# Experts' rows scaled on ScalarE and summed in one reduction; masked attention and quantised layer as one phase

## What is computed

```python
x = x + attn(layernorm(x))             # 16 heads of 8, causal
x = x + cross_attn(layernorm(x), ctx)  # 16 heads of 8, biases
x = x + experts(layernorm(x))          # top 2 of 8: sum of gate_i * expert_i(token)
x = x + rope_attn(layernorm(x)) + bo   # 16 heads of 64, causal, rotary
x = x + masked_attn(layernorm(x), ctx) # 1 head of 128, no weights, causal and padding mask
x = x + quantised_ffn(layernorm(x))

def quantised_ffn(x):                  # inner size 352
    xq = fake_quant(x, clip_x)         # scale = sigmoid(clip) * max|x| / 127 over the whole tensor
    h = fake_quant(silu(xq @ q(w_gate).T) * (xq @ q(w_up).T), clip_down)   # again over the whole tensor
    return h @ q(w_down).T             # q: one scale per row of the weight
```

## Time and profile before

| | |
|---|---|
| median of 3 runs (lowest to highest) | 1297.98 us (1297.2 to 1299.01) |
| the profiled execution's own time | 1297.34 us |
| its span, first to last instruction | 1295.5 us |
| busy: PE, DVE, ACT, POOL | 1035.7, 892.4, 548.0, 549.5 us |
| mean granted PE clock | 0.853 of full speed |

### The profile page before, as it was taken

One profiled execution on the slowest core, in us unless ns is written; L12 is line 12 of the kernel. 1 busy time (PEld: TensorE's weight loads), 2 busy tenths in 40 slices (PEclk: granted clock), 3 DMA queues, 4 the chain that ended last, 5 costly groups with the idle time before them and its releaser, 6 DMA issues. The chain is left out here.

```text
span 1295.5 us, 39531 instructions
## 1 busy us (share of the span) xinstructions
PE 1035.7 (80%) x14827; PEld 838.1 (65%) x14828; DVE 892.4 (69%) x2134; ACT 548.0 (42%) x877; POOL 549.5 (42%) x686
## 2 busy tenths in 40 slices
PE   2999968999935779999975999999999994661453
PEld 1566654666634679999974888888888884441112
DVE  1778764878643934444426999999999986337787
ACT  1556634666511046666632444444444442110343
POOL 3323314434220033333315888888888773103000
PEclk9999976999955579999996999999999998555555
...
DMA packets 33367, 37.54 MB, mean 29 GB/s; under 512 B 6344, under 2 KB 26507, under 8 KB 32908
## 3 DMA queue, kind: packets, MB, share of 16 engines
...
...
## 5 line engine op out<-in xcount | busy, mean ns | idle before, releaser
L1167 POOL DMA_INDIRECT e_x<-xn_rows,e_where x72 | 68.5, 951 | 202.8 <-DVE e_where L1148 116.9
L1137 DVE COPY e_y<-e_Y_ps 128x128 f32<-128x128 f32 x72 | 21.0, 291 | 109.3 <-PE e_Y_ps L1104 109.3
L1324 POOL TENSOR_TENSOR a_E<-a_E,a_rsum 128x512 f32<-128x512 f32 x64 | 66.7, 1042 | 50.7 <-DVE a_rsum L1688 50.7
L262 POOL TENSOR_SCALAR a_KX<-a_KT,a_of_head 128x512 f32<-128x512 f32 x64 | 43.0, 696 | 85.7 <-ACT a_KT L454 85.7
L1094 PE MATMUL e_G_ps<-e_xT,e_gate_here 128*128 128x128 f32 x576 | 77.9, 279 | 0.5 <-ACT e_up_here L1057 0.5
L1094 PE MATMUL e_U_ps<-e_xT,e_up_here 128*128 128x128 f32 x576 | 77.1, 277 | 0.0
L262 POOL TENSOR_SCALAR x_KX<-x_KT,x_of_head 128x512 f32<-128x512 f32 x64 | 43.1, 698 | 78.8 <-issue 49.9
L1104 PE MATMUL e_Y_ps<-m_down_w,e_hT 128*128 x576 | 76.0, 275 | 0.2 <-DVE e_hT L1155 0.2
L1056 ACT ACTIVATE e_gate_here<-m_gate_w 128x512 f32 x72 | 45.4, 630 | 70.7 <-PEq L85 44.9
L1094 PEld LDWEIGHTS e_G_ps<-e_xT,e_gate_here 128*128 128x128 f32 x576 | 71.7, 196 | 0.7 <-ACT e_up_here L1057 0.7
L1094 PEld LDWEIGHTS e_U_ps<-e_xT,e_up_here 128*128 128x128 f32 x576 | 71.2, 194 | 0.0
...
## 6 DMA issues: line engine op xcount, KB each, us to landing
...
```

What stands on the lines that cost most here:

```text
L262: last = nc.gpsimd.tensor_scalar(KX[:, p, :, h * T:(h + 1) * T], src, of_head[:, h:h + 1], 1.0, ALU.mult, ALU.mult)
L1167: nc.gpsimd.indirect_dma_start(out=x[:, j, :], out_offset=None, in_=k.xn_rows, in_offset=bass.IndirectOffsetOnAxis(ap=where[:, j, :], axis ...
L1324: nc.gpsimd.tensor_tensor(e, e, rsum[:, g % 2, :].unsqueeze(2).broadcast_to([P, GH * UB, T]), ALU.mult)\
```

## The change

`X` becomes the first of three planes of one tile, `XR`, each as large as x. Through the mixture phase all phases work in the first plane; from the wide attention on x lies in a tile of its own, `X_of_second_layer`.

In the wide attention ACT scales the gathered rows by their gates into the second and third plane (`apply_gates`, steps 0 and 1, after `evacuate_o`), and DVE sums the three planes of a block into the new x with one `tensor_reduce` whose innermost dimension is the plane (`combine`, step 2). POOL's gathers wait for `gated`, which ACT raises. Before the loop ACT scales the rows of blocks 0 and 1 before its first `normalise`.

The two last phases become `tail_phase` (prefix `t`), all of it written out without loops. Statistics go by block, in two series: series 0 for the masked attention, three blocks ahead, and series 1 for the quantised layer, of a block whose residual has just been added. Normalising moves from DVE to ACT (`centres` on DVE gives its bias), normalising E and quantising the weights go to POOL. Context loads run four blocks ahead, and the weights are loaded between the first and the second of them. In the inner layer POOL quantises x (the first block excepted, which DVE does), ACT, POOL and DVE quantise one chunk of h each, DVE clips, and POOL adds x to the output. PSUM banks of the attention serve the inner layer again, and `HT` lies in the three planes of `XR`.

```diff
@@ wide_attention_phase
-                        pool.wait_ge(combined, (nb - 1) * 2)
+                        pool.wait_ge(gated, (nb - 1) * 2)
...
+            def apply_gates(nb, i, p):
+                act.wait_ge(got[p][i], (nb // 2 + 1) * (16 * UB))
+                for u in range(UB):
+                    rows = k.XR[:, 1 + i, bass.ds(nb * UB + u, 1), :].rearrange("p o c -> p (o c)")
+                    last = nc.scalar.activation(rows, expert_rows[:, p, i, u, :], ACT.Copy, scale=k.gates[:, i, bass.ds(nb * UB + u, 1)])
+                last.then_inc(gated, 1)
...
+                for i in range(2):
+                    apply_gates(0, i, 0)
+                for i in range(2):
+                    apply_gates(1, i, 1)
                 normalise(0)
...
                     evacuate_o(blk, g)
+                    if later(nxt, 2) and g < 2:
+                        apply_gates(blk + 2, g, p)
...
-            def combine(nb, i, p):
-                if i == 1:
-                    wait_here(dve, combined, nb * 2 + 1, passed)
-                dve.wait_ge(got[p][i], (nb // 2 + 1) * (16 * UB))
-                for u in range(UB):
-                    x = k.X[:, nb * UB + u, :]
-                    last = nc.vector.scalar_tensor_tensor(out=x, in0=expert_rows[:, p, i, u, :],
-                                                          scalar=k.gates[:, i, bass.ds(nb * UB + u, 1)], in1=x,
-                                                          op0=ALU.mult, op1=ALU.add)
-                last.then_inc(combined, 1)
+            def combine(nb):
+                wait_here(dve, gated, nb * 2 + 2, passed)
+                rows = k.XR[:, :, bass.ds(nb * UB, UB), :].rearrange("p i u c -> p (u c) i")
+                nc.vector.tensor_reduce(k.X[:, bass.ds(nb * UB, UB), :].rearrange("p u c -> p (u c)"), rows, AX.X, ALU.add)\
+                    .then_inc(combined, 1)
...
-                        if g in (0, 1):
-                            combine(blk + 2, g, p)
+                        if g == 2:
+                            combine(blk + 2)
                         if g == 2:
                             statistics(blk + 2)
@@ masked_attention_phase and quantised_ffn_phase go, tail_phase comes
+    AHEAD = 4
...
+        HT = k.XR[:].rearrange("p i u c -> p i (u c)")
...
+        G_ps = S_ps
+        U_ps = [ET_ps, PV_ps[0]]
+        D_ps = [xT_ps, PV_ps[1]]
...
+            def load_ctx(nb):
+                p = nb % AHEAD
+                if nb >= AHEAD:
+                    sp.wait_ge(pv_ps, nb - AHEAD + 1)
+                sp.dma_start(ctxT[:, p, :], d["ctxT"][:, nb * TOK:(nb + 1) * TOK]).then_inc(ctx_in[p], 16)
+                sp.dma_start(ctxK[:, p, :, :], d["ctxK"][:, nb * BB:(nb + 1) * BB, :]).then_inc(ctx_in[p], 16)
+            sp.dma_start(mask[:], d["mask"]).then_inc(mask_in, 16)
+            load_ctx(0)
+            for w, name in zip(w_rows, ("L1_ffn_w_gate", "L1_ffn_w_up")):
+                for c in range(NC):
+                    sp.dma_start(w[0:ROWS[c], c, :], d[name][c * P:c * P + ROWS[c], :]).then_inc(w_in, 16)
+            sp.dma_start(w_down[:], d["L1_ffn_w_down"]).then_inc(w_in, 16)
+            sp.dma_start(clip[:], d["L1_ffn_clips"]).then_inc(w_in, 16)
+            for nb in range(1, NB):
+                load_ctx(nb)
...
+            def power(s, nb):
+                pool.wait_ge(var_ready[s], nb + 1)
+                if nb >= 1:
+                    pool.wait_ge(xn_ready if s == 0 else XN_ready, nb)
+                nc.gpsimd.tensor_tensor(rstd[s][:], var_eps[s][:], minus_half[:], ALU.pow).then_inc(rstd_ready[s], 1)
+            def normalise_e(nb):
+                pool.wait_ge(rsum_ready, nb + 1)
+                e = E[:, nb % 2]
+                nc.gpsimd.tensor_tensor(e, e, rsum[:, nb % 2, :].unsqueeze(2).broadcast_to([P, UB, T]), ALU.mult)\
+                    .then_inc(en_ready, 1)
...
+            def quantise_x(blk):
+                if blk >= 2:
+                    pool.wait_ge(xq_ready, blk - 1)
+                t = tx[:, blk % 2, :]
+                nc.gpsimd.tensor_scalar(t, XN[:, units(blk), :].rearrange("p u c -> p (u c)"), inv[:, 0:1], MAGIC,
+                                        ALU.mult, ALU.add).then_inc(tx_steps, 1)
+                pool.wait_ge(tx_steps, blk * 2 - 1)
+                nc.gpsimd.tensor_scalar(t, t, MAGIC - QMAX - 1.0, MAGIC + QMAX, ALU.max, ALU.min).then_inc(tx_steps, 1)
+            def quantise_h(blk):
+                if blk >= 2:
+                    pool.wait_ge(hq_ready, blk - 1)
+                nc.gpsimd.tensor_scalar(th[:, blk % 2, TOK:2 * TOK], HT[:, 1, blk * TOK:(blk + 1) * TOK], inv[:, 1:2], MAGIC,
+                                        ALU.mult, ALU.add).then_inc(th_ready[1], 1)
+            def add_residual(blk):
+                pool.wait_ge(y_scaled, blk + 1)
+                y3 = y[:, blk % 2, :].rearrange("p (u c) -> p u c", c=C)
+                nc.gpsimd.tensor_tensor(y3, y3, k.X[:, units(blk), :], ALU.add).then_inc(y_ready, 1)
...
+            power(0, 0)
+            power(0, 1)
+            quantise_rows(0)
+            power(0, 2)
+            quantise_rows(1)
+            normalise_e(0)
+            for blk in range(NB):
+                if blk + 3 < NB:
+                    power(0, blk + 3)
+                if blk + 1 < NB:
+                    normalise_e(blk + 1)
+                if blk >= 1:
+                    power(1, blk - 1)
+                if blk == 1:
+                    quantise_down()
+            power(1, NB - 1)
+            whole(0)
+            pool.wait_ge(scale_steps, 2)
+            for blk in range(1, NB):
+                quantise_x(blk)
+            whole(1)
+            pool.wait_ge(scale_steps, 4)
+            quantise_h(0)
+            quantise_h(1)
+            for blk in range(NB):
+                if blk + 2 < NB:
+                    quantise_h(blk + 2)
+                add_residual(blk)
...
+            def normalise(s, nb):
+                act.wait_ge(centre_ready[s], nb + 1)
+                if s == 0 and nb >= 2:
+                    act.wait_ge(xnT_ps, nb - 1)
+                for u in range(UB):
+                    dst = XN[:, nb * UB + u, :] if s else xn[:, nb % 2, u, :]
+                    last = nc.scalar.activation(dst, k.X[:, nb * UB + u, :], ACT.Identity, bias=centre[s][:, u:u + 1],
+                                                scale=rstd[s][:, u:u + 1])
+                last.then_inc(XN_ready if s else xn_ready, 1)
...
+            for blk in range(NB):
+                evacuate_e(blk)
+                if blk + 1 < NB:
+                    exponentials(blk + 1)
+                if blk + 2 < NB:
+                    evacuate_xT(blk + 2)
+                if blk >= 2:
+                    normalise(1, blk - 2)
+                if blk + 3 < NB:
+                    normalise(0, blk + 3)
...
+            take_magic_x(0)
+            act.wait_ge(gu_ready, 1)
+            evacuate_xq(0)
+            take_magic_x(1)
+            for blk in range(NB):
+                if blk + 1 < NB:
+                    evacuate_xq(blk + 1)
+                silu(blk, 0)
+                if blk + 2 < NB:
+                    take_magic_x(blk + 2)
+                for c in range(1, NC):
+                    silu(blk, c)
+            act.wait_ge(scale_steps, 4)
+            quantise_h(0)
+            quantise_h(1)
+            take_magic_h(0)
+            for blk in range(NB):
+                if blk + 2 < NB:
+                    quantise_h(blk + 2)
+                if blk + 1 < NB:
+                    take_magic_h(blk + 1)
...
+            statistics(0, 0)
+            dve.wait_ge(mask_in, 16)
+            nc.vector.tensor_scalar(pad[:], mask[:], 0.0, NEG, ALU.is_equal, ALU.mult).then_inc(pad_ready, 1)
+            centres(0, 0)
+            statistics(0, 1)
+            centres(0, 1)
+            weight_scales()
+            statistics(0, 2)
+            centres(0, 2)
+            subtract_max(0)
+            sums(0)
+            for blk in range(NB):
+                if blk + 1 < NB:
+                    subtract_max(blk + 1)
+                if blk >= 2:
+                    centres(1, blk - 2)
+                if blk + 3 < NB:
+                    statistics(0, blk + 3)
+                if blk >= 1:
+                    add_residual(blk - 1)
+                if blk + 1 < NB:
+                    sums(blk + 1)
+                if blk >= 3:
+                    magnitude_x(blk - 3)
+                if blk + 3 < NB:
+                    centres(0, blk + 3)
+                if blk >= 1:
+                    statistics(1, blk - 1)
+                if blk == 3:
+                    sigmoids()
+            centres(1, NB - 2)
+            add_residual(NB - 1)
+            statistics(1, NB - 1)
...
+            for blk in range(NB):
+                if blk + 1 < NB:
+                    clip_h(blk + 1)
+                if blk + 2 < NB:
+                    quantise_h(blk + 2)
+                scale_y(blk)
```

(8 more changed lines are left out.)

775 lines of the change are left out of this document (351 added, 424 removed).

## The result

The changed kernel takes 1253.99 us (median of 4 runs, 1252.28 to 1258.19) where the kernel before, run beside it, takes 1298.49 (1297.2 to 1300.1): a ratio of 0.966, 95% interval 0.964 to 0.968. That is 44 us faster where 75 were forecast, and outside the range of 1207 to 1242. The profiled execution took 1253.77, its span is 1251.8.

The account below looks back on a forecast made before the run. VectorE was taken to pace the wide attention, while the masked attention mostly waited, its context loads in the path. Terms -9 - 52.7 + 1.5 - 9.1 - 5.3 = -74.6 from 1297.34 gave 1223 us, range 1207 to 1242.

Parts of the forecast that it names:

- Combining rows: Wide attention, 14 blocks: one reduction replaces VectorE's pairs, block 24.03 to 23.4 us; -9 us in all.
- rivals 1: Wide attention: the reduction costs double, 1.9 instead of 0.96 us, block 24.3, total 1235; chance 0.18.
- 5 (over 6.5): Wide attention: reduction pays per output, kernel slower than before from 6.5 us each, 1321 at 8 us; chance 0.03.
- PE would stall 0.8. Part of that is caught ... I take 0.45: Wide attention, step g = 2: VectorE begins the next step 1.55 us late against 0.75 margin; net TensorE stall 0.45 a block.
- First statistics to first scale: Masked attention merged with the inner layer's preparation: 118.7 us falls to 66, bound by VectorE; -52.7.
- rival 4: Masked attention: context loads still end last, at 9.5 us a block; attention saves 25 less, total 1248; chance 0.03.
- the sign of an error: Merged attention: the forecast is wrong if VectorE idles over 15 us there.
- rival 2: Tail waits between engines: attention iteration 8.5 us instead of 6.9 in five, products wait too; +14, 1237; chance 0.15.
- First scale to first product: Tail, between first scale and first gated product: 6.6 us before, +1.5 for ScalarE's new work and waiting for GpSimd.
- Now ACT takes the second block's subtraction and copy ... and waits for POOL's two quantisings of that block, 0.70 each: Before the first silu: ScalarE's subtraction and copy 0.6 us each, GpSimd's two quantisings 0.70 each, partly overlapped; +1.5.
- Gated products: Inner layer's products: 44.3 us falls to 35.2, 4.4 a block, with the quantisings moved to GpSimd; -9.1.
- Down projection: Last stage: 3.64 us a block falls to 3.0, quantising and adding moved off VectorE; -5.3 over eight blocks.

Follow-up runs that it names:

- experiments 1 and 2: Changed kernel with rows combined as before: 0.9627 of the kernel before; changed kernel with the sum one step earlier and ScalarE's scalings ahead of its output copy: 0.9541.
- experiments 5 and 6: Changed kernel with the three-plane reduction done twice at g = 2: 0.9700 of before; same doubling in the kernel with the sum at g = 1: 0.9623.
- experiment 9: On top of experiment 4, GpSimd quantises the inner layer's weights in iterations 1 to 3 of the merged attention, not ahead of the loop: 0.9419 of before.
- experiment 12: On top of experiment 4, the residual in the down projection is added by VectorE instead of GpSimd: 0.9430 of the kernel before.
- experiment 4: Changed kernel with the sum one step earlier and the two maxima over partitions by TensorE instead of GpSimd: 0.9406 of before, median 1216.42 us.

## Why the prediction was wrong

In the order of its steps.

- **Combining rows: wrong, -9 against +4.8.** (To the tail's first statistics it is +5.6, of which 0.8 stand ahead of the phase.) The reduction was put at 0.96 and took 1.02; rivals 1 (1.9) and 5 (over 6.5) fell. What failed is the step "PE would stall 0.8. Part of that is caught ... I take 0.45": PE loses 1.45 a block (24.39 - 22.94). The extras of the step were 2.94, not 2.4, since the epsilon took 0.93 (it was put at up to 0.50) and the sum, the statistics and their aggregates wait for one another 0.15 each. DVE began the row maxima 2.08 late (scores done at 872.60, start at 874.68). I had named the wrong waiter: not the transposes behind the products of the keys, but the weighing of values behind those of the queries, which end 2.67 after the row maxima begin and had room for 1.34 of lateness, less 0.31 until PE goes on: 2.08 - 1.03 = 1.05, the step's loss. PE waits there for ACT's copy of the values as well, which ended 0.04 before the products of the queries; it stands behind exponentials that had waited 2.37 for DVE, so both come from the same lateness. The 1.05 is not caught either: PE is the bound, and it loses another 0.35 right behind this weighing (877.66 to 878.53, where other steps take 0.52). That all of it hangs on the placing is shown by experiments 1 and 2; how much lateness a step may have, experiments 5 and 6 showed me to have understood only in part.
- **First statistics to first scale: nearly right, 69.3 against 66.** No wait for context is left, so rival 4 fell. Before the loop it takes 14.9, forecast 14.7. From the first row maxima to the first scale it takes 54.4 against 49.5 (42.9 + 6.6). DVE is idle 20.6 of the 69.3 us, more than the 15 that I had named as the sign of an error: the excess stands mostly in the first iteration, 7.5 us where I had 3.6 (1110.48 to 1118.00), which waits 1.74 for exponentials and 2.84 for scores. This is rival 2 (waits between queues), at a quarter of its 14 us. Moving POOL's work into later iterations did not win it back (experiment 9).
- **First scale to first product: wrong, 17.5 against 8.1.** The step that failed is "Now ACT takes the second block's subtraction and copy ... and waits for POOL's two quantisings of that block, 0.70 each". I priced POOL's operations and not what stands between two of them: 3.0 more until the scale (3.73 after DVE's maximum, where it is 0.73 at the second one), 7 until POOL quantises again, and the second of the two quantisings is 1.97, not 0.70. With the maxima by TensorE the stretch is 8.9. That PE's and ACT's queues with block 0 ahead of block 1 would have hidden part of the 7 us was not tried.
- **Gated products: right, a little better.** 32.5 against 35.2: 4.1 a block instead of 4.4.
- **Down projection: per block right, the stretch wrong.** 3.02 a block, forecast 3.0, for the reason given (DVE and POOL hold one another up, experiment 12). But the stretch is 38.8, not 32.4, for POOL's 7.05 after the second all-reduce. Without it: 32.6.

With both faults mended (experiment 4) the wide attention's stretch of row maxima is 364.9, 11.3 under before, and the others are 69.9, 8.9, 32.5 and 32.6. Beside the forecast's 9 less, 66, 8.1, 35.2 and 32.4 that is right to 4 us in each, for a kernel without the two faults. That the five together come out within 0.1 us is luck: 2.3 and 2.7 us better in two, 3.9, 0.8 and 0.2 worse in the others. The forecast's rivals were all prices of single operations or waits between queues; that an engine stops between two instructions of its own was among neither the terms nor the rivals, though the name of the all-reduce stood in the diff with POOL's new work right behind it.
